# Second attention layer's edge loop: a group's sums split around the transpositions, rescaling put ahead of the key product

## Chip, cores and metric

One core of one Trainium2 chip runs the whole program in one launch. The metric is the device time of one execution in microseconds (us), smaller is better; it is given as the median of several executions. Engines are named as in the profile: PE (TensorE matmul; PEld is its weight load), DVE (VectorE), ACT (ScalarE), POOL (GpSimd), SP (SyncE and its DMA queue).

## What is computed

The program is a graph network of four residual layers over 3125 nodes of 256 features and 50,000 edges sorted by target node. The change is in the third, an attention over edges (in the kernel it is the second graph layer):

```python
qkv = (h @ W_qkv + b_qkv).reshape(n, 3, H, DH)          # H = 8 heads of DH = 32
q, k, v = (qkv[:, 0], qkv[:, 1], qkv[:, 2])
score = jnp.einsum('ehd,ehd->eh', q[dst], k[src]) * SCALE
mx = jax.ops.segment_max(score, dst, num_segments=n)
ex = jnp.exp(score - mx[dst])
denom = jax.ops.segment_sum(ex, dst, num_segments=n)
attn = ex / denom[dst]
msg = attn[:, :, None] * v[src]
h_new = jax.ops.segment_sum(msg, dst, num_segments=n)
...
return (h_out + h) @ W_out + b_out
```

## The kernel before

`attention_edges` goes over the edges in tiles of 128. Two tiles are an item, which sums into one window of 128 target nodes; two items (four tiles) are a group; there are 110 groups. Four groups are a chunk: over its 2048 edges the running maximum of the scores is made at one time, so that a chunk's weights are known only some steps after its scores. A node whose edges cross from one chunk to the next has its sums rescaled to the new maximum.

Each engine has a program of its own, written by hand as a function `step`, which `rounds` writes out once for each step i (a function `at(k)` gives the group i+k). What one engine's step does is done in exactly that order, and the engines meet at semaphores (`need` waits for several). The place of a step is i mod 4. In step i:

- POOL gathers key and value rows of group i+3 by four indirect DMAs (L1772), once the slot of group i-7 has been summed.
- ACT copies the two window sums of group i-8 out of PSUM (`keep`, L1787; the second copy waits for the first), with the gather indices of group i+4 (L1816) between the two copies; then it makes the one-hot matrix of group i+3 (L1826, L1828: distance, then a ramp) and turns the transposed one-hot of group i+2 into the operand `a_spread` (L1833). At place 2 it spreads the weights (`weights`, L1801) and copies the factor of growth (L1836); at place 1 it takes the exponentials (L1840, L1842).
- PE makes the queries of the edges of group i+1 (the query products, L1898 and L1899, two for each of four tiles; they need `a_spread`), transposes the one-hot of group i+2 (L1912), and sums group i-7 (`add_group`): it clears two PSUM banks with products of zeros (L1862) and adds four tiles (L1865). The sums wait for the group's messages (`s_msg`) and for both copies of the group summed one step earlier (`s_acc`), because the banks change owner. Ahead of the last tile's query products stands one small product of the chunk (`chunk_rows`): at place 0 the transposition of the scores (L1873), at place 1 the carries (L1877), at place 2 the transposition of the exponentials (L1881). Behind the transpositions stand at place 0 the tails (L1917, which needs DVE's ends, L1964) and at place 2 the growth (L1921). At place 3 the group summed is the first of its chunk, and the sums wait for DVE's rescaling too (`s_rs`).
- DVE multiplies queries and keys of group i (key product, L2005), then reduces the products to scores (L2018), and weights the values of group i-6 (messages, L1954). The chunk's scans stand between (L1962 to L1964 and L1971 to L1973 at place 0, L1980 to L1986 at place 1). At place 3 the rescaling (L1993, L1995) stands behind the key product; it works on a PSUM bank and waits for the copies of the group summed one step earlier.

At each end, POOL, ACT and PE run a few steps with less work (filling, and draining the last eight groups).

Of the kernel before, what the change touches and what calls it, by code (L numbers as in the profile page):

```python
# [283 lines left out]
def real(g):  # L284

    return not isinstance(g.n, int) or 0 <= g.n < g.COUNT
# [1419 lines left out]
def attention_edges(c, A):  # L1706
# [10 lines left out]
    with ExitStack() as s:  # L1717
# [21 lines left out]
        bank = lambda w: ap[:, bass.ds(w & 1, 1), 0:DM].rearrange("p a d -> p (a d)")  # L1739
        other = lambda w: ap[:, bass.ds((w + 1) & 1, 1), 0:DM].rearrange("p a d -> p (a d)")  # L1740
        hT = c.ps("a_hotT", [P, IG * P], F32, s)
# [11 lines left out]
        with nc.Block() as block:  # L1753
# [23 lines left out]
            def _(act):  # L1777
# [28 lines left out]
                def step(at):  # L1806
                    i = at(0)
                    a = at(-SUM - 1)
                    if real(a):
                        wins = item_windows(act, c, a.n)  # L1810
                        keep(a, 0, wins[0])
                    g = at(4)
                    if real(g):

                        need(act, s_ag, (s_rows[g.slot], g.turn * 64))
                        nc.scalar.copy(idx[:, g.slot, :], c.src_i[:, bass.ds(g.n * IG, IG)]).then_inc(s_idx, 1)  # L1816
                    if real(a):
                        keep(a, 1, wins[1])
                    if i.place == 2 and closed(i.chunk - 1):
# [31 lines left out]
            def _(pe):  # L1851
# [4 lines left out]

                def add_group(m, both):

                    wins = both >> 1, (both + 1) >> 1
                    need(pe, None, (s_msg, m.n + 1), (s_acc, m.n * JG), *([(s_rs, 2 * m.chunk + 2)] if m.place == 0 else []), own=True)  # L1860
                    for w in [p for p in previous] + [wins[0]]:
                        mm(other(w)[:, 0:2], none[:, :], none[:, 0:2], start=True, stop=False, skip_group_check=True)  # L1862
                    previous[:] = [wins[1]]
                    for j in range(IG):
                        last = mm(bank(wins[j // CT]), hot[:, hots(m, j), :], rows[:, m.slot * IG + j, D:ROW], start=False, stop=False, skip_group_check=True)  # L1865
                    last.then_inc(s_agg, 1)

# [15 lines left out]
                def step(at):  # L1883
                    i = at(0)
                    ch = i.chunk - 1
                    m = at(-SUM)
                    sums = ahead.take(i.step, "sums", m.n) if real(m) else None
                    g = at(1)
                    if real(g):

                        both = ahead.take(i.step, "q", g.n)
                        wins = both >> 1, (both + 1) >> 1
                        need(pe, None, (s_sp, g.n + 1), (s_pr, g.n - 1), own=True)
                        for j in range(IG):
                            if j == IG - 1:
                                chunk_rows(i, ch)
                            both_parts = window(c.qhl, wins[j // CT])
                            mm(qp[g.pair][:, j * D:(j + 1) * D], spread[:, g.pair, j, :], both_parts[:, 0:D], start=True, stop=False)  # L1898
                            last = mm(qp[g.pair][:, j * D:(j + 1) * D], spread[:, g.pair, j, :], both_parts[:, D:2 * D], start=False, stop=True)  # L1899
                        last.then_inc(s_q, 1)  # L1900
                    else:
                        chunk_rows(i, ch)
                    if real(at(2)):
                        ahead.fetch(i.then, "q", at(2).n)
# [3 lines left out]
                    if real(h):  # L1908
# [4 lines left out]
                        last.then_inc(s_ht, 1)  # L1913
                    if i.place == 0 and closed(ch):

                        need(pe, None, (s_en, ch + 1), own=True)
                        mm(tails, c.rows_of_head[:, :], ends[:, :, :].rearrange("p a t -> p (a t)"), start=True, stop=True).then_inc(s_tl, 1)  # L1917
                    if i.place == 2 and closed(ch):
# [3 lines left out]
                    if real(m):  # L1922
                        add_group(m, sums)
                pe.wait_ge(s_none, 1)
# [4 lines left out]
            def _(dve):  # L1929
# [67 lines left out]
                def step(at):  # L1997
                    i = at(0)
                    m = at(-LAG)
                    ch = i.chunk - 1  # L2000
                    if real(i):

                        need(dve, s_dg, (s_q, i.n + 1), (s_rows[i.slot], (i.turn + 1) * 64))
                        keys = rows[:, four(i), 0:D]
                        v.tensor_tensor(keys, qp[i.pair][:, :].rearrange("p (a d) -> p a d", a=IG), keys, ALU.mult).then_inc(s_pr, 1)  # L2005
# [4 lines left out]
                    if i.place == 1 and closed(ch):  # L2010
                        chunk_peaks(ch)
                    if i.place == 3 and closed(ch):
                        rescale(i, ch)
                    if real(m) and i.place != 2:
                        message(m)
                    if real(i):
                        need(dve, s_dg, (s_pr, i.n + 1))
                        v.tensor_reduce(sc[:, i.cslot, i.place * IG:(i.place + 1) * IG, :].rearrange("p t h -> p (t h)"),  # L2018
                                        rows[:, four(i), 0:D].rearrange("p t (h d) -> p t h d", h=H), AX.X, ALU.add).then_inc(s_sc, 1)
                    if real(m) and i.place == 2:  # L2020
                        message(m)
                    if i.place == 0 and closed(ch):
# [464 lines left out]
```

## Time and profile before

| What | us |
|---|---|
| Median of 3 runs | 2123.23 |
| Lowest and highest run | 2111.26 and 2154.74 |
| The profiled execution, its own time | 2139.3 |
| Span of its trace | 2137.6 |
| Sums (L1865), first and last start | 1283.0 and 1901.5 |
| Key products (L2005), first and last start | 1245.8 and 1850.1 |

Busy shares of the whole span are PE 82%, DVE 70%, ACT 54% and POOL 53%. They are means over phases with different limits and say little here; the phase of the change is read for itself. All times in the trace are us from the start of the span. A row of the timeline gives the start, the busy time, the engine, the line, what is written from what, and in brackets how long the engine had been idle before it and what ended that. Ends of matmuls are modelled, so one PE row can reach a little into the next.

### The profile page before, as it was taken

The page shows a single profiled execution, that of the slowest core. Times are in us where ns is not written, and L with a number is a line of the kernel's source. Part 1 is how long each engine was busy: PE and PEld are TensorE (multiplying, and loading weights), DVE is VectorE, ACT ScalarE, POOL GpSimd, SP SyncE. Part 2 cuts the span into 40 slices and gives each one's busy share as a digit, 9 for nine tenths or more (in the row PEclk, how much of TensorE's full clock was granted, in tenths as well). Part 3 has the DMA queues.
Part 4 walks back from the last instruction along what each step waited for, and adds up shares of the span by engine and source line. Part 5 has one row for each costly group of instructions (what it writes and reads, how often), then busy time and mean ns, then how long its engine had stood idle before and what let it go on. Part 6 is the DMA issues. An engine that isn't in the chain of part 4 may idle for free. (4 is left out here: it accounts for less than half of the span.)

```text
span 2137.6 us, 44266 instructions
## 1 busy us (share of the span) xinstructions
PE 1752.7 (82%) x10497; PEld 1546.7 (72%) x10498; DVE 1487.7 (70%) x3008; ACT 1145.9 (54%) x2630; POOL 1130.8 (53%) x1194
## 2 busy tenths in 40 slices
PE   3699999999999989828974958888888888766268
PEld 3499999999999969718963747766766766645267
DVE  4388888888888845544545848889887777637722
ACT  1677777777777726403421255666665555326133
POOL 0376666666666601562443667777776666312012
PEclk7799999999999989759986959999998888767589
DMA  2443333333333312233323667677766666323310
GB/s 93 135 120 106 107 108 104 107 108 104 107 108 104 100 31 82 73 121 103 117 72 109 208 188 198 199 201 202 203 190 185 175 176 179 100 64 118 128 48 29
DMA packets 132555, 267.74 MB, mean 125 GB/s; under 512 B 24029, under 2 KB 75887, under 8 KB 132406
## 3 DMA queue, kind: packets, MB, share of 16 engines
q0 software_dynamic: 63456, 191.61, 30.8%
q1 hardware_dynamic: 68534, 73.21, 11.0%
q8 instruction: 64, 1.05, 0.2%
q10 hardware_dynamic: 416, 1.18, 0.2%
q14 instruction: 85, 0.70, 0.1%
HBM read 225.34 MB, written 42.50 MB: 125 GB/s over the span
## 5 line engine op out<-in xcount | busy, mean ns | idle before, releaser
L319 POOL DMA_INDIRECT e_rows<-h_table,e_idx x440 | 452.3, 1028 | 216.7 <-issue 107.3
L1772 POOL DMA_INDIRECT a_rows<-kv_table,a_idx x440 | 435.2, 989 | 173.9 <-issue 170.6
L1865 PE MATMUL a_agg<-a_rows,x 128*128 128x264 f32 x880 | 271.0, 460 | 0.1
L619 PE MATMUL e_w<-w2h,e_hidl 128*128 128x256 f32 x880 | 248.4, 305 | 2.9 <-DVE e_msg L704 2.9
L589 PE MATMUL e_agg<-e_msg,e_hot 128*128 128x256 f32 x880 | 246.7, 403 | 0.0
L620 PE MATMUL e_w<-w2l,e_hidh 128*128 128x256 f32 x880 | 227.1, 280 | 0.0
L1787 ACT COPY sums<-a_agg x220 | 83.3, 379 | 261.1 <-PE a_agg L1865 229.4
L1865 PEld LDWEIGHTS a_agg<-a_rows,x 128*128 128x128 f32 x880 | 182.7, 218 | 35.4
L704 DVE TENSOR_TENSOR e_msg<-e_w,e_rows 128x1024 f32<-128x1024 f32 x110 | 134.7, 1225 | 94.8 <-PE e_w L623 94.8
L619 PEld LDWEIGHTS e_w<-w2h,e_hidl 128*128 128x128 f32 x880 | 166.4, 189 | 14.6 <-issue 5.2
L623 PE MATMUL e_w<-w2h,e_hidh 128*128 128x256 f32 x880 | 175.3, 280 | 0.0
L639 ACT COPY sums<-e_agg x220 | 80.8, 367 | 173.0 <-PE e_agg L589 173.0
L620 PEld LDWEIGHTS e_w<-w2l,e_hidh 128*128 128x128 f32 x880 | 166.4, 189 | 6.1
L1898 PE MATMUL a_q<-q_parts,a_spread 128*128 x440 | 162.2, 388 | 8.5 <-ACT a_spread L1833 7.0
L1954 DVE TENSOR_TENSOR a_rows<-a_rows 128x256 f32<-128x256 f32 x440 | 156.8, 416 | 6.2 <-ACT a_rows L1801 5.7
L589 PEld LDWEIGHTS e_agg<-e_msg,e_hot 128*128 128x128 f32 x880 | 151.0, 191 | 11.7
L2005 DVE TENSOR_TENSOR a_rows<-a_q,a_rows 128x1024 f32<-128x1024 f32 x110 | 133.0, 1209 | 28.0 <-DMA a_rows<-kv_table,a_idx 23.0
L1826 ACT ACTIVATE a_apart<-iota_n,dst_rel 128x128 f32<-128x128 f32 x440 | 140.5, 394 | 0.0
L674 DVE TENSOR_TENSOR e_hidl<-e_hid,e_hidh 128x1024 fp32r<-128x1024 f32 x110 | 135.0, 1227 | 3.4
L2018 DVE TENSOR_REDUCE a_sc<-a_rows 128x32 f32<-128x1024 f32 x110 | 133.3, 1212 | 5.1 <-DVE a_rows L2005 1.1
L691 DVE SCALAR_TENSOR_TENSOR e_hid<-e_soft,e_z 128x1024 f32<-128x1024 f32 x110 | 133.1, 1210 | 5.3 <-ACT e_soft L659 5.3
L623 PEld LDWEIGHTS e_w<-w2h,e_hidh 128*128 128x128 f32 x880 | 135.2, 189 | 0.0
(461 smaller groups left out, 4512.2 us busy)
## 6 DMA issues: line engine op xcount, KB each, us to landing
e_ea<-in_eaT SPq DMA_DIRECT2D x220, 64.0 KB
m_rows<-expert_rows SPq DMA_DIRECT2D x32, 272.0 KB, 2.7
e_rows<-h_table,e_idx POOLq DMA_INDIRECT x440
a_rows<-kv_table,a_idx POOLq DMA_INDIRECT x440, 3.7
q_ab<-expert_out SPq DMA_DIRECT2D x50, 128.0 KB
kv_table<-q_kv SPq DMA_DIRECT2D x25, 256.0 KB, 2.2
u_stage<-in_m_w SPq DMA_DIRECT2D x16, 256.0 KB
x<-in_x SPq DMA_DIRECT2D x1, 3200.0 KB, 14.9
```

What stands on the lines that cost most here:

```text
L319: c.nc.gpsimd.indirect_dma_start(out=rows[:, g.slot8, j, :], out_offset=None, in_=table, in_offset=bass.IndirectOffsetOnAxis(ap=idx[:, g.s ...
L589: last = mm(bank(wins[j]), hot[:, g.slot4, t, :], msg[:, g.slot4, t, :], start=False, stop=False, skip_group_check=True)
L619: mm(w, hidl[:, g.slot, cols[k]], w2h[:, k, :], start=(k == 0), stop=False)
L620: mm(w, hidh[:, g.slot4, cols[k]], w2l[:, k, :], start=False, stop=False)
L623: last = mm(w, hidh[:, g.slot4, cols[k]], w2h[:, k, :], start=False, stop=(k == KC - 1))
L674: low = lambda to, x, h: v.tensor_tensor(to, x, h.bitcast(F32), ALU.subtract)
L704: v.tensor_tensor(msg[:, g.slot4, :, :], wp[:, :].rearrange("p (a d) -> p a d", a=IG), rows[:, g.slot8, :, :], ALU.mult).then_inc(s_msg, 1)
L1772: nc.gpsimd.indirect_dma_start(out=rows[:, g.slot * IG + j, 0:2 * D], out_offset=None, in_=c.kv_dram, in_offset=bass.IndirectOffsetOnAxis( ...
L1826: nc.scalar.activation(apart[:, j, :], c.iota_n[:, :], ACT.Abs, bias=c.dst_rel[:, bass.ds(g.n * IG + j, 1)], scale=-1.0).then_inc(s_ap, 1)
L1865: last = mm(bank(wins[j // CT]), hot[:, hots(m, j), :], rows[:, m.slot * IG + j, D:ROW], start=False, stop=False, skip_group_check=True)
L1898: mm(qp[g.pair][:, j * D:(j + 1) * D], spread[:, g.pair, j, :], both_parts[:, 0:D], start=True, stop=False)
L1954: last = v.tensor_tensor(values, values, ex, ALU.mult)
```

## The change

On PE, `add_group` becomes `add_items`, which can do the first item's two tiles, the second's, or both. At places 0, 1 and 2 the clears and the first item's sums now stand between the query products and the transpositions, and the second item's sums behind them. The wait for messages and copies (`group_ready`) goes along, and stands ahead of the last tile's query products. At place 0 the tails move behind the transpositions to directly ahead of the second item's sums. At place 3 all sums stay behind the transpositions. On DVE the rescaling of place 3 stands ahead of the key product, and at place 2 the messages stand ahead of the reduction, as at the other places. On ACT the gather indices are copied ahead of both sum copies.

```diff
 # ACT, step
+                    g = at(4)
+                    if real(g):
+                        need(act, s_ag, (s_rows[g.slot], g.turn * 64))
+                        nc.scalar.copy(idx[:, g.slot, :], ...).then_inc(s_idx, 1)
                     a = at(-SUM - 1)
                     if real(a):
                         wins = item_windows(act, c, a.n)
-                        keep(a, 0, wins[0])
-                    g = at(4)
-                    ...
-                    if real(a):
-                        keep(a, 1, wins[1])
+                        for j in range(JG):
+                            keep(a, j, wins[j])
 # PE
+                def group_ready(m):
+                    need(pe, None, (s_msg, m.n + 1), (s_acc, m.n * JG), own=True)
+                def add_items(m, both, items, tails_of):
+                    wins = both >> 1, (both + 1) >> 1
+                    held = wins[0] & 1, wins[1] & 1
+                    if 0 in items:
+                        emptied = previous + [(wins[0] + 1) & 1]
+                        previous[:] = [(wins[1] + 1) & 1]
+                        if m.place == 0:
+                            pe.wait_ge(s_rs, 2 * m.chunk + 2)
+                        for b in emptied:
+                            mm(at_bank(b)[:, 0:2], none[:, :], none[:, 0:2], start=True, stop=False, skip_group_check=True)
+                    if tails_of is not None:
+                        chunk_tails(tails_of)
+                    for j in [j for t in items for j in range(t * CT, (t + 1) * CT)]:
+                        last = mm(at_bank(held[j // CT]), hot[:, hots(m, j), :], rows[:, m.slot * IG + j, D:ROW], start=False, stop=False, skip_group_check=True)
+                    if 1 in items:
+                        last.then_inc(s_agg, 1)
 # PE, step
+                    first_now = real(m) and m.place != 0
                         for j in range(IG):
                             if j == IG - 1:
                                 chunk_rows(i, ch)
+                                if first_now:
+                                    group_ready(m)
                             ...
+                    if first_now:
+                        add_items(m, sums, [0], None)
                     ...
                     if real(m):
-                        add_group(m, sums)
+                        if not first_now:
+                            group_ready(m)
+                        add_items(m, sums, [1] if first_now else [0, 1], tails_of)
+                    elif tails_of is not None:
+                        chunk_tails(tails_of)
 # DVE, step
+                    if i.place == 3 and closed(ch):
+                        rescale(i, ch)
                     if real(i):
                         ...
-                    if i.place == 3 and closed(ch):
-                        rescale(i, ch)
-                    if real(m) and i.place != 2:
+                    if real(m):
                         message(m)
                     if real(i):
                         ...
-                    if real(m) and i.place == 2:
-                        message(m)
```

Engine PE at place 0, before, from the last tile's query products on. `m_rows4` and `m_out0` are the names under which the listing has the semaphores of the messages (`s_msg`) and of the copies (`s_acc`); `a_ends` is set by DVE's ends, and L343 loads the next windows' numbers.

```order
L1873 MATMUL a_misc<-ident,a_sc 128x128 [waits a_grown,e1_acc]
L1898 MATMUL a_q<-q_parts,a_spread 128x256
L1899 MATMUL a_q<-q_parts,a_spread 128x256
...
L1912 MATMUL a_hotT<-ident,x 128x128 [waits e1_w,e1_hidhigh]
L1912 MATMUL a_hotT<-ident,x 128x128 x3
L1917 MATMUL a_misc<-a_ends,rows_of_head 8x32 [waits a_ends]
L1862 REGISTER_ALU [waits m_out0,m_rows4]
...
L1865 MATMUL a_agg<-a_rows,x 128x264 x2
```

The same place with the change:

```order
L1888 MATMUL a_misc<-ident,a_sc 128x128 [waits a_grown,e1_acc]
L1916 MATMUL a_q<-q_parts,a_spread 128x256 [waits m_out0,m_rows4]
L1917 MATMUL a_q<-q_parts,a_spread 128x256
L1875 REGISTER_ALU x2
...
L1879 MATMUL a_agg<-a_rows,x 128x264 x2
...
L1934 MATMUL a_hotT<-ident,x 128x128 [waits e1_w,e1_hidhigh]
L1934 MATMUL a_hotT<-ident,x 128x128 x3
L1859 MATMUL a_misc<-a_ends,rows_of_head 8x32 [waits a_ends]
...
L1879 MATMUL a_agg<-a_rows,x 128x264 x2
```

The wait for messages and copies moved up past the four transpositions and the last pair of query products, and the tails moved down past half of the sums.

Engine DVE from the key product of place 2 to the reduction of place 3, before (`a_ex` is set by the spread weights, `a_grown` by ACT's copy of the growth):

```order
L2005 TENSOR_TENSOR a_rows<-a_q,a_rows 128x4x256 [waits e1_msg,e1_rows4]
...
L2018 TENSOR_REDUCE a_sc<-a_rows 128x32 [waits e1_agg]
L1954 TENSOR_TENSOR a_rows<-a_rows 128x256 [waits a_ex]
L1954 TENSOR_TENSOR a_rows<-a_rows 128x256 x3
L2005 TENSOR_TENSOR a_rows<-a_q,a_rows 128x4x256 [waits e1_msg,e1_rows5]
L1993 REGISTER_ALU [waits a_grown,m_out0]
...
L1993 SCALAR_TENSOR_TENSOR a_agg<-a_grown,a_agg 128x256
```

The same stretch with the change:

```order
L2030 TENSOR_TENSOR a_rows<-a_q,a_rows 128x4x256 [waits e1_msg,e1_rows4]
...
L1977 TENSOR_TENSOR a_rows<-a_rows 128x256 [waits a_ex]
L1977 TENSOR_TENSOR a_rows<-a_rows 128x256 x3
L2041 TENSOR_REDUCE a_sc<-a_rows 128x32 [waits e1_agg]
L2016 REGISTER_ALU [waits a_grown,m_out0]
...
L2016 SCALAR_TENSOR_TENSOR a_agg<-a_grown,a_agg 128x256
...
L2030 TENSOR_TENSOR a_rows<-a_q,a_rows 128x4x256 [waits e1_msg,e1_rows5]
```

The rescaling, with its wait for the copies, moved ahead of a key product, and the messages of place 2 ahead of a reduction.

## Rows read from the trace of the kernel before

**Rows 1.** Windows: us, busy us of PE, PEld, DVE, ACT, POOL; PEclk; DMA share; GB/s.

```profile
1292.90:1850.10 557.20, 474.80 (x2395) 387.33 (x2394) 464.90 (x1003) 330.98 (x1041) 393.46 (x397) 0.92 0.67 189
1611.30:1826.40 215.10, 184.05 (x866) 150.00 (x865) 167.47 (x362) 120.91 (x380) 144.60 (x145) 0.86 0.63 178
1754.00:1756.00 2.00, 2.00 (x6) 1.46 (x6) 1.70 (x5) 0.00 (x0) 0.49 (x1) 0.50 0.76 184
1771.00:1773.00 2.00, 2.00 (x6) 1.46 (x6) 1.34 (x2) 0.00 (x0) 0.82 (x1) 0.50 0.70 193
```

**Rows 2.** Line L1993, one rescaling per chunk, in the first two stretches of rows 1.

```profile
L1993 DVE SCALAR_TENSOR_TENSOR a_agg<-a_grown,a_agg x25: 414/429/430, 1304.5 to 1839.6; 128x256 f32 x25
L1993 DVE SCALAR_TENSOR_TENSOR a_agg<-a_grown,a_agg x9: 414/428/430, 1624.9 to 1815.9; 128x256 f32 x9
```

**Rows 3.** Waits of PE, 1283 to 1905: us in total, times, longest.

```profile
PE a_agg L1862 <- DVE a_agg L1995: 36.7, 28, 2.8
PE a_misc L1917 <- DVE a_ends L1964: 24.1, 27, 1.6
```

**Rows 4.** Timeline, PE and ACT, a step of place 1.

```profile
1482.87 0.47 PE L1898 MATMUL a_q<-q_parts,a_spread 128*128 x1
1483.30 0.28 PE L1898 MATMUL a_q<-q_parts,a_spread 128*128 x1
1484.36 0.38 ACT L1787 COPY sums<-a_agg  x1 [0.28 <-issue]
1484.62 0.63 PE L1912 MATMUL a_hotT<-ident,x 128*128 128x128 f32 x4
1485.18 0.27 PE L1862 MATMUL a_agg<-a_none 128*128 128x2 f32 x1
1485.82 2.04 PE L1865 MATMUL a_agg<-a_rows,x 128*128 128x264 f32 x8
```

**Rows 5.** Timeline, PE and ACT, the next step, of place 2.

```profile
1487.50 0.48 PE L1898 MATMUL a_q<-q_parts,a_spread 128*128 x1
1488.99 0.38 ACT L1787 COPY sums<-a_agg  x1 [0.28 <-issue]
1489.82 0.38 PE L1921 MATMUL a_misc<-a_diag,a_first 8*128 8x8 f32 x2
```

**Rows 6.** Timeline, PE, ACT and DVE, the step of place 3.

```profile
1492.45 0.48 PE L1898 MATMUL a_q<-q_parts,a_spread 128*128 x1
1493.48 1.22 DVE L2005 TENSOR_TENSOR a_rows<-a_q,a_rows 128x1024 f32<-128x1024 f32 x1
1493.98 0.38 ACT L1787 COPY sums<-a_agg  x1 [0.20 <-issue]
1494.73 0.43 DVE L1993 SCALAR_TENSOR_TENSOR a_agg<-a_grown,a_agg 128x256 f32 x1
1495.68 0.62 PE L1862 MATMUL a_agg<-a_none 128*128 128x2 f32 x2 [1.03 <-DVE a_agg L1995]
```

**Rows 7.** Timeline, PE and ACT, the step of place 0 and the next start.

```profile
1499.43 0.38 ACT L1787 COPY sums<-a_agg  x1 [0.27 <-issue]
1500.68 0.23 PE L1917 MATMUL a_misc<-a_ends,rows_of_head 128*8 128x32 f32 x2 [0.90 <-DVE a_ends L1964]
1501.12 0.61 PE L1862 MATMUL a_agg<-a_none 128*128 128x2 f32 x2 [0.21 <-issue]
1503.37 0.48 PE L1898 MATMUL a_q<-q_parts,a_spread 128*128 x1
```

**Rows 8.** Timeline, draining: the second copy and the rescaling behind it.

```profile
1889.65 0.38 ACT L1787 COPY sums<-a_agg  x1 [0.37 <-ACT sums L1787]
1890.40 0.43 DVE L1993 SCALAR_TENSOR_TENSOR a_agg<-a_grown,a_agg 128x256 f32 x1 [4.43 <-issue]
```

**Rows 9.** Timeline, filling: the spread and the query product waiting for it.

```profile
1249.24 0.58 ACT L1833 CAST a_spread<-a_hotT 128x512 fp32r<-128x512 f32 x1 [1.25 <-PE a_hotT L1912]
1250.02 0.58 PE L1898 MATMUL a_q<-q_parts,a_spread 128*128 x1 [0.93 <-ACT a_spread L1833]
```

More of the change, by code:

```diff
@@ L1739, in attention_edges @@
         bank = lambda w: ap[:, bass.ds(w & 1, 1), 0:DM].rearrange("p a d -> p (a d)")
-        other = lambda w: ap[:, bass.ds((w + 1) & 1, 1), 0:DM].rearrange("p a d -> p (a d)")
+        at_bank = lambda b: ap[:, bass.ds(b, 1), 0:DM].rearrange("p a d -> p (a d)")
         hT = c.ps("a_hotT", [P, IG * P], F32, s)
@@ L1807, in step @@
                     i = at(0)
-                    a = at(-SUM - 1)
-                    if real(a):
-                        wins = item_windows(act, c, a.n)
-                        keep(a, 0, wins[0])
                     g = at(4)
@@ L1816, in step @@
                         nc.scalar.copy(idx[:, g.slot, :], c.src_i[:, bass.ds(g.n * IG, IG)]).then_inc(s_idx, 1)
+                    a = at(-SUM - 1)
                     if real(a):
-                        keep(a, 1, wins[1])
+                        wins = item_windows(act, c, a.n)
+                        for j in range(JG):
+                            keep(a, j, wins[j])
                     if i.place == 2 and closed(i.chunk - 1):
@@ L1855, in _, with chunk_tails @@
                 previous = []
-                def add_group(m, both):
-                    wins = both >> 1, (both + 1) >> 1
[L1860 to L1866, printed above, removed]
+                def chunk_tails(ch):
+                    need(pe, None, (s_en, ch + 1), own=True)
+                    mm(tails, c.rows_of_head[:, :], ends[:, :, :].rearrange("p a t -> p (a t)"), start=True, stop=True).then_inc(s_tl, 1)
+                def group_ready(m):
+                    need(pe, None, (s_msg, m.n + 1), (s_acc, m.n * JG), own=True)
+                def add_items(m, both, items, tails_of):
+                    wins = both >> 1, (both + 1) >> 1
+                    held = wins[0] & 1, wins[1] & 1
[12 more added lines that the diff above has]
+                        last.then_inc(s_agg, 1)
                 def chunk_rows(i, ch):
@@ L1902, in step @@
                         chunk_rows(i, ch)
+                        if first_now:
+                            group_ready(m)
+                    if first_now:
+                        add_items(m, sums, [0], None)
                     if real(at(2)):
@@ L1913, in step @@
                         last.then_inc(s_ht, 1)
-                    if i.place == 0 and closed(ch):
-                        need(pe, None, (s_en, ch + 1), own=True)
-                        mm(tails, c.rows_of_head[:, :], ends[:, :, :].rearrange("p a t -> p (a t)"), start=True, stop=True).then_inc(s_tl, 1)
+                    tails_of = ch if i.place == 0 and closed(ch) else None
                     if i.place == 2 and closed(ch):
@@ L1922, in step @@
                     if real(m):
-                        add_group(m, sums)
+                        if not first_now:
+                            group_ready(m)
+                        add_items(m, sums, [1] if first_now else [0, 1], tails_of)
+                    elif tails_of is not None:
+                        chunk_tails(tails_of)
                 pe.wait_ge(s_none, 1)
```

## Prediction

> **What bounds the kernel now.** I first read the busy time by stretches. From the key product at 1292.9 to the one at 1850.1 the trace has 557.20 us [rows 1], and in it 25 rescalings, one per chunk [rows 2]: 22.29 us a chunk on average. That mean hides two kinds of chunk. In the nine chunks from 1611.3 to 1826.4 [rows 1, 2] a chunk takes 215.10 / 9 = 23.90 us, and PE's granted clock is 0.86 on average. As the clock has only the levels 1.2 and 2.4 GHz, 0.86 means 28% of the time at the lower one, 6.7 us of each chunk; the reader sees two such stretches, at 1754 and at 1771, with PE busy all the time at 0.50 [rows 1]. An undisturbed chunk, from the query products of one place 1 to those of the next, takes 1503.37 - 1482.87 = 20.50 us [rows 4, 7]. So a chunk with two falls of the clock costs 3.40 us more than one with none, 1.70 us a fall.
>
> Next come PE's waits. In this phase it waits 36.7 us for the rescaling (28 times) and 24.1 us for the ends (27 times) [rows 3]. These two are what the change goes for. To see whether removing them shortens a chunk I read the timeline of one undisturbed chunk, step by step. There a third wait shows that has no line of its own in the list of waits: at place 1 the second copy out of PSUM ends at 1484.36 + 0.38 = 1484.74, and the first clear starts at 1485.18, 0.44 behind it [rows 4]. The query products and the transpositions (1484.62 to 1485.18) just fill the time until the copies are done. So the loop from the sums over the two copies to the next sums is already closed at this place; all PE work in front of the clears is free because it lies under the copies.
>
> **The change part by part.** No computation is added or removed; only order and waits change.
>
> *First item ahead of the transpositions, places 0, 1, 2.* The wait for the copies now stands ahead of the last pair of query products. What lay under the copies, that pair and the four transpositions, comes behind them. I count one step from the end of the second copy, at the full clock, with these pieces: from a copy's end to a waiting query product 0.20 us (from the spread's end, 1249.24 + 0.58 = 1249.82, to the product at 1250.02 [rows 9]); a pair of products at the head of a stream 0.43 (1482.87 to 1483.30); clears 0.64 (1485.18 to 1485.82); all four tiles of sums 1.68 (1485.82 to 1487.50), so 0.84 an item; transpositions 0.56 [rows 4, 5].
>
> - Place 1: 1484.74 + 0.20 + 0.43 + 0.64 + 0.84 + 0.56 + 0.84 = 1488.25, where the next step started at 1487.50 before: 0.75 later. But the next query products also need the spread of these transpositions, which now come late. They start at 1486.85 and end 0.63 later [rows 4] at 1487.48; in the filling steps, where PE has nothing else, it is idle for 0.93 us between the transpositions and the query product that needs their spread [rows 9]. That gives 1488.41, 0.91 later, and it is the later one that counts.
> - Place 2: the second copy ends at 1488.99 + 0.38 = 1489.37 [rows 5]. With the growth between (0.38) the step ends at 1489.37 + 0.20 + 0.43 + 0.64 + 0.84 + 0.56 + 0.38 + 0.84 = 1493.26, against 1492.45 [rows 6]: 0.81 later. The spread is no later than this.
> - Place 0: the copy ends at 1499.81; with the tails, 1500.68 to 1501.12 or 0.44 [rows 7], the step ends at 1499.81 + 0.20 + 0.43 + 0.64 + 0.84 + 0.56 + 0.44 + 0.84 = 1503.76, against 1503.37: 0.39 later. Here the old wait of 0.90 for the ends does go: DVE's ends come before 1500.68, and PE is at the tails only at about 1502.5. Most of the gain is eaten by what now follows the copies.
>
> *Rescaling ahead of the key product, place 3.* The key product ended at 1493.48 + 1.22 = 1494.70 and the rescaling started at 1494.73, so it looks as if the key product held it. But the second copy ended at 1493.98 + 0.38 = 1494.36, and 0.37 later is 1494.73 [rows 6]. In the draining steps, where no key product stands in between, the rescaling starts 0.37 behind the copy too (1889.65 + 0.38 = 1890.03, then 1890.40 [rows 8]). So the copy holds it, the move gains nothing here, and the wait of 1.03 us on PE stays: 0. The key product itself, 1.22 us, now lies behind the rescaling; the scores' transposition at place 0 gets later by at most that, mostly under the new wait for the copies. That wait is at least 0.78 us: at place 1, three pairs at 0.43 from 1482.87 end at 1484.16, and PE goes on at 1484.94. So 0.44 at most can stick out; I take 0 and keep 0.44 for the bounds. Without that cover it would be the whole 1.22.
>
> *Messages of place 2 ahead of the reduction, indices ahead of the copies.* Both 0. The weights they need are spread on ACT right behind the second copy (1489.37), while DVE's key product of place 2 runs; the index copy leaves a gap on ACT that the second copy cannot use, since it is held by the first one (0.37 idle there without an index copy [rows 8]). POOL's gathers get their semaphore a little earlier and still wait for the end of the sums. Filling and draining steps are left as they are: there the sums already wait for copies.
>
> Sum for a chunk at the full clock: 0.91 + 0.81 + 0 + 0.39 = 2.11, so 22.61 us. The bounds: the step after the copies may take 0.44 as before the clears instead of 0.20, which adds 3 x 0.24 = 0.72 (23.33, and 23.77 with the 0.44 above); or the last pair may be hidden wholly, which takes off 3 x 0.43 = 1.29 (21.32). I take 0.20, since there a query product waits for ACT, as it now will.
>
> *The clock.* PE's waits before were two, near each other, at places 3 and 0. Now there are four, one in each step: the old 1.03 at place 3, and some 0.8 us at each of the other places. In the late stretch the clock fell twice a chunk with two waits hardly larger than these; in the undisturbed chunk it did not fall. Spread evenly, each wait is alone, but there are more. I take one fall a chunk, between the none of the undisturbed chunk and the two of the late ones, at 1.70 us: 22.61 + 1.70 = 24.31.
>
> On this the row shows PE at 0.50 at 1771, right behind a wait for the rescaling and so for a copy [rows 1]. The Trainium skill (TensorE: Matmul & The Clock Gate, section "Loop structure matters more than you think") has it that a copy out of PSUM between streams of matmuls doesn't break PE's warmth, by which there would be no falls and the first rival's time. The same page ("A second HAM failure mode: psum-queue depth-cycling") says that small idles between groups of matmuls, coming often, make the clock swing between its levels; that would give falls as in the forecast or in the second rival. The trace agrees with the second statement: 0.86 over nine chunks, with no wait on PE longer than 2.8 us.
>
> The time: 25 chunks at 24.31 are 607.8 us instead of 557.2, so 50.6 more. On the profiled execution's 2139.3 us (its span of 2137.6 and 1.7 around it, which stay) that is 2190 us. The runs shown have a median of 2123.23, some 16 us under the profiled one; as the new phase is built up from its own chunks and not from the mean of before, I stay with 2190.
>
> **Rivals.**
>
> 1. *No falls.* The waits are short and far apart, and the clock stays full. Then a chunk is 22.61, 25 are 565.3, 8.1 more: 2147 us, between 2115 (21.32 a chunk) and 2176 (23.77). For it: the undisturbed chunk had waits of 1.03 and 0.90 at the full clock. Against it: the nine late chunks had hardly longer ones and fell twice each.
> 2. *Two falls a chunk.* The waits come at every step and the late stretch's pattern holds throughout: 22.61 + 3.40 = 26.01, 25 are 650.3, 93.1 more: 2232 us.
> 3. *Not slower: the copies are not what ends last.* If the copies ended 0.8 us or more earlier against PE's products than in the timeline [rows 4, 5, 7], the moved wait would find them done; the ends' wait of 0.90 would be gone, and without the pair of waits the clock would stay full. Then every chunk is 20.50 or a little less, 25 are 512.5, 44.7 less: 2095 us. For it speaks that both waits it goes for are large [rows 3]. Against it: the clear at 1485.18 stands 0.44 behind the copy, so the copies have no slack at all. It decides from the point where the second copy ends before the third tile's products do.
>
> **How the numbers follow.** The forecast, about one fall a chunk, gets 0.45; no falls 0.25; two or more falls 0.18; the copies in time 0.12. The time given is 2190 us. The range 2125 to 2240 takes in most of the first rival and the second rival, and leaves out the third and what is beyond two falls. About 2% can be told from no change in this kernel: against 2123 that is 2081 to 2166. Slower: the forecast nearly whole (0.42) and the second rival, 0.60. Within 2%: the first rival, the rest of the forecast and two thirds of the third, 0.36. Faster: 0.04.
>
> **What would show it.** In the profile after, the timeline of a chunk should show the last pair of query products starting some 0.2 us behind the second copy at places 0, 1 and 2, with PE idle for 0.8 us or more before it; a new entry in PE's waits, query products (L1916) for ACT's copies; the entry of the tails for the ends gone; the rescaling still some 0.37 behind the second copy. The chunk should be 22 to 23 us where the clock stays full. The forecast is wrong if query products do not wait there, if an undisturbed chunk is 20.5 us or less, or if the falls come four times a chunk or not at all.

## The result, and the profile after

The median is 2175.86 us (2174.38 to 2178.78, 4 runs), beside 2127.45 for the kernel before on the same chip: a ratio of 1.0224 [1.0165, 1.0282]. In brackets stands the 95% interval of a ratio. It is slower; whether by 2% or more the interval leaves open. The profiled execution took 2175.47 us, its span is 2173.7, so 36.1 us more than before. The first row below is the window between the same two key products as in [rows 1], the second one undisturbed chunk, from the query products of place 1 to the next of place 1.

```profile
1288.40:1886.90 598.50, 482.17 (x2390) 366.35 (x2390) 461.31 (x1003) 337.63 (x1041) 399.39 (x398) 0.96 0.62 176
1480.68:1503.86 23.18, 18.40 (x99) 14.01 (x97) 18.47 (x40) 13.77 (x42) 15.94 (x17) 1.00 0.62 182
```

The phase grew from 557.20 to 598.50 us, 41.3 more; it starts 4.5 us earlier, and what comes behind it is 0.7 shorter: 36.1. A chunk takes 598.50 / 25 = 23.94 us on average, with 24.31 predicted. The mean clock rose from 0.92 to 0.96 all the same, so the loss is in the order. The nine chunks at the full clock average 23.41 us (before: 20.59, also nine), the sixteen others 24.24.

The waits of PE in this phase, as in [rows 3]:

```profile
PE a_q L1916 <- ACT sums L1787: 51.1, 76, 1.1
PE a_hotT L1934 <- issue: 31.9, 93, 0.6
PE a_agg L1875 <- DVE a_agg L2018: 27.2, 27, 2.8
```

The ends' 24.1 us are gone from the list. In their place the query products wait 51.1 us for the copies, 76 times, and the wait for the rescaling has stayed. The second row was not predicted: before the transpositions PE is idle 93 times with nothing to wait for ("issue").

The timeline of place 1 in the undisturbed chunk, PE and ACT, answers to [rows 4]; the last four rows are places 2 and 0 ([rows 5, 7]):

```profile
1480.68 0.44 PE L1916 MATMUL a_q<-q_parts,a_spread 128*128 x1
1482.13 0.38 ACT L1787 COPY sums<-a_agg  x1 [0.37 <-ACT sums L1787]
1482.65 0.36 PE L1916 MATMUL a_q<-q_parts,a_spread 128*128 x1 [0.61 <-ACT sums L1787]
1482.97 0.61 PE L1875 MATMUL a_agg<-a_none 128*128 128x2 f32 x2
1483.53 1.15 PE L1879 MATMUL a_agg<-a_rows,x 128*128 128x264 f32 x4
1485.10 0.63 PE L1934 MATMUL a_hotT<-ident,x 128*128 128x128 f32 x4 [0.42 <-issue]
1486.65 0.38 PE L1916 MATMUL a_q<-q_parts,a_spread 128*128 x1
...
1489.32 1.15 PE L1879 MATMUL a_agg<-a_rows,x 128*128 128x264 f32 x4
1490.83 0.63 PE L1934 MATMUL a_hotT<-ident,x 128*128 128x128 f32 x4 [0.36 <-ACT x L1827]
...
1500.89 1.15 PE L1879 MATMUL a_agg<-a_rows,x 128*128 128x264 f32 x4
1502.31 0.63 PE L1934 MATMUL a_hotT<-ident,x 128*128 128x128 f32 x4 [0.26 <-issue]
```

The second copy ends at 1482.13 + 0.38 = 1482.51 and the waiting query product starts 0.14 later, after 0.61 us of idle time. From the start of the first item's sums to the transpositions it is 1485.10 - 1483.53 = 1.57 us at place 1, 1.51 at place 2 and 1.42 at place 0, where the prediction had 0.84. (At place 2 the trace names ACT's one-hot, L1827, as what came last, at 1489.86 + 0.63 = 1490.49; the loads of that step, of the kind shown below for the other two, close at 1490.6. Over the phase the one-hot is named 6 times, for 2.2 us.) What fills that time is on PE's sequencer. L343, a helper, loads the next step's window numbers into registers; the code has it between the first item's sums and the transpositions. Its rows in this chunk's place 1, then at place 0 (durations in ns, first and last start in us):

```profile
L343 PEldq TENSOR_LOAD <-g_row x2: 298/300/302, 1483.5 to 1484.3; - x2
L343 PEldq FUSED_REGOPS  x2: 151/151/151, 1483.9 to 1484.7; - x2
L343 PEldq SEQ_ASSERT  x2: 18/18/18, 1484.1 to 1484.9; - x2
...
L343 PEldq TENSOR_LOAD <-g_row x2: 296/298/301, 1500.9 to 1501.6; - x2
```

And in the kernel before, at place 1 of [rows 4]:

```profile
L343 PEldq TENSOR_LOAD <-g_row x2: 301/302/302, 1483.2 to 1483.9; - x2
L343 PEldq FUSED_REGOPS  x2: 151/151/151, 1483.6 to 1484.2; - x2
```

Before, the two loads ran from 1483.2 to about 1484.4, while the query products ran and the copies were pending (the second ended at 1484.74): hidden. After, the sequencer stands at the moved wait until 1482.51, so the loads start only at 1483.5 and end at 1484.9, and the transpositions behind them start at 1485.10. Before, "issue" ahead of the transpositions was 11.7 us in 38 times.

At place 3 the rescaling answers to [rows 6]:

```profile
1493.99 0.38 ACT L1787 COPY sums<-a_agg  x1 [0.37 <-ACT sums L1787]
1494.74 0.43 DVE L2016 SCALAR_TENSOR_TENSOR a_agg<-a_grown,a_agg 128x256 f32 x1 [3.51 <-ACT sums L1787]
1495.73 0.61 PE L1875 MATMUL a_agg<-a_none 128*128 128x2 f32 x2 [0.83 <-DVE a_agg L2018]
```

It starts 0.37 behind the copy as before, though no key product stands in front of it now; DVE is idle 3.51 us ahead of it.

### The profile page after: what moved, and what is told of

Same layout as the page of the kernel before. It is cut to its first block and busy times, and to the rows that moved or that the text cites. A ratio compares the mean times of both kernels' runs of the same rounds, so it can differ in the third digit from the quotient of the medians.

```text
span 2173.7 us, 44266 instructions
## 1 busy us (share of the span) xinstructions
PE 1754.3 (81%) x10497; PEld 1522.3 (70%) x10498; DVE 1481.4 (68%) x3008; ACT 1153.4 (53%) x2630; POOL 1138.1 (52%) x1194
## 5 line engine op out<-in xcount | busy, mean ns | idle before, releaser
L1772 POOL DMA_INDIRECT a_rows<-kv_table,a_idx x440 | 440.0, 1000 | 208.1 <-issue 205.1
L1916 PE MATMUL a_q<-q_parts,a_spread 128*128 x440 | 147.3, 356 | 62.3 <-ACT sums L1787 51.1
L1879 PEld LDWEIGHTS a_agg<-a_rows,x 128*128 128x128 f32 x880 | 169.4, 210 | 29.0 <-issue 0.2
L589 PEld LDWEIGHTS e_agg<-e_msg,e_hot 128*128 128x128 f32 x880 | 149.9, 190 | 11.5
L1916 PEld LDWEIGHTS a_q<-q_parts,a_spread 128*128 128x128 f32 x440 | 90.1, 205 | 90.6 <-issue 85.7
```

Of the source, the lines that this page charges most:

```text
L589: last = mm(bank(wins[j]), hot[:, g.slot4, t, :], msg[:, g.slot4, t, :], start=False, stop=False, skip_group_check=True)
L1772: nc.gpsimd.indirect_dma_start(out=rows[:, g.slot * IG + j, 0:2 * D], out_offset=None, in_=c.kv_dram, in_offset=bass.IndirectOffsetOnAxis( ...
L1879: last = mm(at_bank(held[j // CT]), hot[:, hots(m, j), :], rows[:, m.slot * IG + j, D:ROW], start=False, stop=False, skip_group_check=True)
```

## The experiments

The kernel before ran on the chip of each set: 2133.04 (first four runs), 2126.51 (next four), 2133.63 (last three). All ratios are to it unless said otherwise. The change itself was not run again beside them, so its 2175.86 us is from another set of runs. Where a run is given as a share of the change, times of two sets are divided. A chunk counts as one at the full clock if its granted clock is 0.99 or more from the key product of one place 1 to the next.

**PE's part alone.** `add_items`, the moved wait and the tails as in the change; ACT and DVE as before.

```diff
 # against the change: ACT, step
-                        for j in range(JG):
-                            keep(a, j, wins[j])
+                        keep(a, 0, wins[0])
...
+                        keep(a, 1, wins[1])
 # DVE, step
-                    if i.place == 3 and closed(ch):
-                        rescale(i, ch)
...
-                    if real(m):
+                    if i.place == 3 and closed(ch):
+                        rescale(i, ch)
+                    if real(m) and i.place != 2:
                         message(m)
...
+                    if real(m) and i.place == 2:
+                        message(m)
```

> PE's part of the change alone; ACT and DVE in the old order. Theory 1 (the wait for the copies, moved ahead of the last pair of query products, is the whole loss): as the full change, 1.018 to 1.027 of the kernel before, an undisturbed chunk 23.2 to 23.8 us, PE's query products waiting some 50 us for ACT's copies. Theory 2 (DVE loses: its key product and scores come late behind the rescaling): most of the loss gone, 1.000 to 1.008.

Measured: 2176.61 us, 1.0208 [1.0137, 1.0280]; full-clock chunks 23.04, mean 23.98; PE waits 50.5 us for the copies. In the time, PE's part is the whole loss. A full-clock chunk is a little shorter than I had expected, and 0.37 shorter than in the full change.

**The rest alone.** The order of ACT (indices ahead of both copies) and DVE as in the change, PE as before.

```diff
 # DVE, step
+                    if i.place == 3 and closed(ch):
+                        rescale(i, ch)
...
-                    if i.place == 3 and closed(ch):
-                        rescale(i, ch)
-                    if real(m) and i.place != 2:
+                    if real(m):
                         message(m)
...
-                    if real(m) and i.place == 2:
-                        message(m)
 # ACT, step: as in the change
```

> ACT's and DVE's part of the change alone (indices ahead of the copies, rescaling ahead of the key product, messages ahead of the reduction at place 2); PE in the old order. Theory 1: 0.995 to 1.005 of the kernel before, the rescaling still 0.37 us behind the second copy, PE's wait for the rescaling still about 1 us each time. Theory 2: 1.010 to 1.022. A third view (the key product held the rescaling): PE's wait for the rescaling down by half or more, 0.98 to 0.99.

Measured: 2147.15 us, 1.0056 [1.0024, 1.0088]; the two full-clock chunks of its profile 21.12. The profiled execution is the slowest of the ten, 2159.97. PE's wait for the rescaling is 34.2 us in 27 times, hardly less than the 36.7 before, so the key product did not hold the rescaling. A small loss, not the nothing that I had put down; the run on the rescaling below goes into it.

**Loads early.** The change, with PE's loads of the next step's windows moved ahead of the wait, so that they run under it. `fetch_next` holds the four lines taken out below.

```diff
                             if j == IG - 1:
+                                fetch_next()
                                 chunk_rows(i, ch)
...
                         add_items(m, sums, [0], None)
-                    if real(at(2)):
-                        ahead.fetch(i.then, "q", at(2).n)
-                    if real(at(1 - SUM)):
-                        ahead.fetch(i.then, "sums", at(1 - SUM).n)
```

> The full change, with PE's loads of the next step's window numbers moved from between the first item's sums and the transpositions to ahead of the wait for the copies. Theory 1a (the 0.6 to 0.7 us per step by which the new step is longer than predicted is PE's queue executing these loads behind the wait): the gap between the first item's last sum and the transpositions falls from about 0.7 us to under 0.2, an undisturbed chunk from 23.4 to 21.4 to 22.2 us, 0.975 to 0.988 of the full change. Theory 1b (the transpositions wait for something else there, such as ACT's one-hot): 0.995 to 1.005 of the full change, the gap stays.

Measured: 2145.46 us, 1.0052 [1.0021, 1.0083], so 2145.5 / 2175.9 = 0.986 of the change. Full-clock chunks 21.87 instead of 23.41. A place 0 at the full clock, then the loads in the step behind it:

```profile
1492.45 0.36 PE L1922 MATMUL a_q<-q_parts,a_spread 128*128 x1 [0.78 <-ACT sums L1787]
1493.36 1.15 PE L1879 MATMUL a_agg<-a_rows,x 128*128 128x264 f32 x4
1494.35 0.60 PE L1937 MATMUL a_hotT<-ident,x 128*128 128x128 f32 x4
1497.62 0.40 PE L1892 MATMUL a_misc<-carried,heads_of_row 8*128 8x34 f32 x2 [0.72 <-issue]
...
L343 PEldq TENSOR_LOAD <-g_row x2: 300/301/302, 1496.3 to 1497.0; - x2
```

The first item takes 0.99 us to the transpositions, not 1.42. The loads run while the copies are pending (the second ends at 1497.71 in that step), and "issue" now stands ahead of the chunk's product. This one line of order is worth 1.54 us of a chunk's 2.82 of growth.

**Tails alone.** The kernel before; only the tails move, from ahead of the clears to between the two items' sums.

```diff
                     for j in range(IG):
+                        if j == CT and tails_of is not None:
+                            chunk_tails(tails_of)
                         last = mm(bank(wins[j // CT]), ...)
...
-                    if i.place == 0 and closed(ch):
-                        need(pe, None, (s_en, ch + 1), own=True)
-                        mm(tails, ...).then_inc(s_tl, 1)
+                    tails_of = ch if i.place == 0 and closed(ch) else None
```

> The kernel before, with only the tails of place 0 moved: from ahead of the clears to between the two items' sums; nothing goes ahead of the transpositions. Theory 1: the wait for the ends (24 us in all) goes without anything new in its place, and the clock falls less often, as the pair of waits is broken up: 0.975 to 0.992 of the kernel before. Rival (DVE's own chain sets the chunk, 20.5 us at best, and the falls come from the wait for the rescaling alone): 0.995 to 1.003.

Measured: 2105.93 us, 0.9886 [0.9816, 0.9955]; mean chunk 21.22, full-clock chunks 20.72, seventeen of them instead of nine. The ends' wait is gone, the rescaling's is unchanged:

```profile
1286.80:1817.40 530.60, 448.61 (x2390) 362.56 (x2390) 463.10 (x1003) 332.51 (x1040) 401.36 (x398) 0.97 0.70 199
...
PE a_agg L1867 <- DVE a_agg L2001: 35.2, 27, 2.8
```

A full-clock chunk is no shorter than before (20.59): what is gained is the clock, 0.97 for 0.92. One of the two waits that stood near each other is gone; that the falls are fewer for this reason is an argument here, and the next run tests it. So one part of the change pays by itself. Whether it still does beside the others was not tried.

**Before, with PE kept busy.** The transpositions of places 0 and 3, just ahead of the two waits, are done three times.

```diff
+                        for again in range(3 if i.place in (0, 3) else 1):
                             for j in range(IG):
                                 last = tr(hT[:, j * P:(j + 1) * P], ...)
```

> The kernel before, with the four transpositions of places 3 and 0 done three times in a row instead of once; same values, 16 additional transpositions a chunk that lie where PE would wait for the rescaling and for the ends. Theory C (the late stretch's 23.9 us a chunk come from the clock, and the clock falls because of PE's idle time at these two places): the time at the lower clock in the 25 chunks falls from some 90 us to under 25, all chunks at 20.4 to 21.0 us, 0.978 to 0.988 of the kernel before. Rival D (transpositions don't count for the clock, or the falls have another cause): low time as before, 0.998 to 1.010.

Measured: 2097.00 us, 0.9880 [0.9813, 0.9947]. The clock is full in 24 of the 25 chunks, the mean chunk 20.74:

```profile
1281.30:1799.70 518.40, 477.74 (x2787) 398.39 (x2786) 465.00 (x1002) 330.24 (x1041) 393.53 (x398) 1.00 0.70 203
```

PE's idle time at the two waits fell from 36.7 to 8.5 us (rescaling) and from 24.1 to 4.4 (ends). Only filler was added, and the falls are gone: in the kernel before, PE's idle time at these waits caused them. The two places were filled together, so this run does not tell which of them counts for more.

**The change, with PE kept busy.** The third tile's query products are done three more times ahead of the wait, at places 0 to 2.

```diff
                                 if first_now:
+                                    for again in range(3):
+                                        mm(qp[g.pair][:, (j - 1) * D:j * D], ...)
+                                        mm(qp[g.pair][:, (j - 1) * D:j * D], ...)
                                     group_ready(m)
```

> The full change, with the third tile's query products repeated three times at places 0, 1 and 2 just ahead of the wait for the copies; same values, filling PE's new idle time of about 0.7 us. Theory C: the time at the lower clock in the 25 chunks falls from 51 us to under 20, the mean chunk from 23.94 to about 23.4 (what an undisturbed one takes already), 0.990 to 0.996 of the full change, so still 1.010 to 1.020 of the kernel before: the order, not the clock, is most of the loss. Rival D: low time unchanged, 0.998 to 1.006 of the full change.

Measured: 2171.90 us, 1.0224 [1.0156, 1.0292], so 0.998 of the change (by their two ratios to the kernel before, 1.000). That is in the rival's range and not in the one forecast. PE's wait for the copies fell from 51.1 to about 1 us, full-clock chunks rose from nine to fifteen, and still they take 23.36 us:

```profile
1286.90:1882.80 595.90, 527.95 (x2840) 413.55 (x2840) 462.27 (x1001) 337.30 (x1039) 395.39 (x398) 0.97 0.62 177
...
PE a_hotT L1937 <- issue: 31.5, 94, 0.6
PE a_agg L1875 <- DVE a_agg L2021: 27.0, 27, 2.8
```

Ten chunks are still disturbed, more than I had expected; PE's waits for the rescaling and for the loads, the last two rows, are left, which may be why. But most of the time lost is not the clock's: with the clock fuller, the chunk stays as long.

**Wait behind the last pair.** The change, with the wait behind the last pair of query products, and the loads between that pair and the wait.

```diff
-                                if first_now:
-                                    group_ready(m)
...
                         ahead.fetch(i.then, "sums", at(1 - SUM).n)
+                    if first_now:
+                        group_ready(m)
+                        add_items(m, sums, [0], None)
```

> The full change, with the wait for messages and copies moved behind the last pair of query products, and PE's loads of the next window numbers between that pair and the wait. Theory 1: pair (0.32 us a step) and loads (about 0.6) come back under the copies, only clears, first item and transpositions stay behind: an undisturbed chunk 21.0 to 21.7 us, 0.972 to 0.986 of the full change, 0.995 to 1.006 of the kernel before. Rival (the loads alone mattered): not under 21.8 us a chunk, as with the loads moved.

Measured: 2148.58 us, 1.0104 [1.0023, 1.0184]; full-clock chunks 22.44, longer than expected and on the rival's side of 21.8. What is missing is at the wait. A second copy and the clears behind it, in the timeline of ACT and PE, then the loads of that step:

```profile
1465.43 0.38 ACT L1787 COPY sums<-a_agg  x1 [0.37 <-ACT sums L1787]
1466.62 0.61 PE L1875 MATMUL a_agg<-a_none 128*128 128x2 f32 x2 [1.16 <-ACT sums L1787]
...
L343 PEldq TENSOR_LOAD <-g_row x2: 294/298/302, 1464.9 to 1465.5; - x2
L343 PEldq SEQ_ASSERT  x2: 18/18/18, 1465.5 to 1466.1; - x2
```

From the copy's end (1465.81) to the clears it is 0.81 us, in the two steps behind it 0.44 and 0.59, while a query product waiting at the same semaphore starts after 0.14. Two things make up the difference. The loads start only behind the last pair and here close at 1466.1, some 0.35 after the copy, so part of them still sticks out. And the clears have register instructions of their own behind the wait: these are the 0.44 that is left where the loads end before the copy, as at the next wait.

**Rescaling alone.** The kernel before, with only the rescaling ahead of the key product.

```diff
+                    if i.place == 3 and closed(ch):
+                        rescale(i, ch)
                     if real(i):
...
-                    if i.place == 3 and closed(ch):
-                        rescale(i, ch)
```

> The kernel before with nothing but the rescaling moved ahead of the key product. Theory R (with PE's old order, where no new wait covers it, the 0.6 % that the ACT and DVE parts cost is the key product and the scores behind it coming late): 1.003 to 1.009 of the kernel before, an undisturbed chunk 21.0 us. Rival (the messages of place 2 or the indices cost it): 0.998 to 1.002, an undisturbed chunk 20.5 us.

Measured: 2138.08 us, 1.0028 [1.0004, 1.0053]; full-clock chunks 21.05, 0.46 longer than before. In the old order of PE the key product behind the rescaling is late for what follows: in a full-clock chunk the tails of place 0 start 1459.15 - 1455.87 = 3.28 us into the step, against 1500.68 - 1497.94 = 2.74 in the kernel before. By the time the loss is 4.5 us, where 25 x 0.46 would be 11.5; in the profiles 13 chunks of 25 were disturbed instead of 16. As PE's part alone (2176.61) and the whole change (2175.86) agree, no cost of the move shows in the time under the new wait. Their full-clock chunks (23.04 and 23.41) leave up to some tenths of a us open.

**Short copy.** The change, with a shorter second copy.

```diff
+                    lo = D if j == 1 else 0
-                    nc.scalar.copy(window(c.sums, w)[:, 0:DM], bank(w)).then_inc(s_acc, 1)
+                    nc.scalar.copy(window(c.sums, w)[:, lo:DM], ap[...]).then_inc(s_acc, 1)
```

> The full change, with the second copy out of PSUM cut from 264 to its last 8 columns, so that most of the second item's sums are left out of the result. The copy lasts about 0.17 instead of 0.38 us and nothing else changes. Theory 1 (the loop from the sums over both copies to the next sums sets the step): 0.2 us less a step, an undisturbed chunk 0.7 to 0.9 us shorter, 22.5 to 22.8 us, 0.985 to 0.994 of the full change. Rival (PE's own work, or the spread, sets it): a chunk within 0.2 us of 23.4, 0.998 to 1.002.

Measured: 2157.23 us, 1.0128 [1.0082, 1.0175], so 0.991 of the change; full-clock chunks 22.74, which is 0.67 less; PE's wait for the copies 40.4 us. The copy is 0.17 instead of 0.38 us, 0.21 shorter. It counts in all four steps, since at place 3 the rescaling waits for it, so 0.84 could be gained. Counted from PE's query products, the steps of the full-clock chunks are on average 0.10, 0.17, 0.17 and 0.13 shorter at places 1, 2, 3 and 0, 0.57 in all by these borders of a chunk. So a chunk follows the end of the second copy, though not to the full length: PE's waits for ACT's one-hot, 2.2 us in the change, are 7.0 here.

**Tails alone, with filler.** Two ways to hold the clock on top of the moved tails: the third tile's query products four more times at place 3, or the transpositions of place 3 three times.

```diff
+                                for again in range(4 if i.place == 3 and real(m) else 0):
+                                    mm(qp[g.pair][:, (j - 1) * D:j * D], ...)
 # the other
+                        for again in range(3 if i.place in (3,) else 1):
```

> The kernel before with the tails between the two items' sums, as in the earlier run, and at place 3 the third tile's query products repeated four times while PE would wait for the rescaling; same values. Theory C: the wait for the rescaling is what still makes the clock fall there; the mean chunk goes from 21.2 to 20.5 us, low time in the 25 chunks under 10 us, 0.975 to 0.986 of the kernel before. Rival D: as without the repetition, 0.985 to 0.992.

> The kernel before with the tails between the two items' sums, and at place 3 the four transpositions done three times while PE would wait for the rescaling; same values. Theory C: no falls are left between the filling and the draining steps (low time in the 25 chunks under 8 us), the mean chunk 20.4 to 20.7 us, 0.980 to 0.988 of the kernel before. Rival (DVE's chain of 20.5 us and more is all that is left, and the two steps don't add up): 0.987 to 0.991, as each of them alone.

Measured: 2101.51 us, 0.9888 [0.9821, 0.9954], with the query products, and 2100.63 us, 0.9865 [0.9831, 0.9900], with the transpositions. The mean chunks are 21.08 and 20.93 (tails alone: 21.22), at the full clock 20.77 and 20.80. The first run is in its rival's range; both mean chunks are longer than expected, with five and three chunks disturbed. The second has the lowest ratio of all, 1.35% under the kernel before, but by the intervals no filler is told apart from the tails alone.

## Why the prediction was right, and where its terms were off

It said slower, 2190 us, range 2125 to 2240; it is 2175.86. The mechanism is the one named: the wait for the copies out of PSUM moved ahead of work that had lain under them, and that work came behind it. "No slack at all" holds at place 1, where it was read; at place 0 the first clear stood at 1501.12, 1.31 behind the copy's end and not 0.44, and the prediction's sum for that step has this in it. Products waiting some 0.2 us behind the copy, their new entry in PE's waits, the ends' entry gone and the rescaling 0.37 behind the copy all show as stated. Two terms were mis-sized, in opposite directions: the chunk at the full clock came out 0.80 longer, its clock term 1.17 smaller. That the mean chunk, 23.94, came within 0.37 of 24.31 is so in part luck.

- *The chunk at the full clock*: 22.61 predicted, 23.41 measured. The term that was off is "0.84 an item", from the first item's sums to the transpositions: it took 1.42 to 1.57. The prediction counted matmuls and left out the two register loads that stand in that place of the program. From the copy's end to the transpositions it had 0.20 + 0.43 + 0.64 + 0.84 = 2.11; it was 2.59, 2.53 and 2.46 at places 1, 2 and 0, although wake-up, pair and clears came out shorter (0.14, 0.32, 0.56 at place 1). Moving the loads away took 1.54 us off a chunk. Over whole steps it is place 1 that misses most: the steps grew by 1.34, 0.90, -0.01 and 0.45 us at places 1, 2, 3 and 0, against 0.91, 0.81, 0 and 0.39.
- *The spread chain* at place 1: 0.93 predicted between transpositions and next query product; 1485.10 + 0.63 = 1485.73 to 1486.65 is 0.92.
- *The clock*: 1.70 us a chunk predicted, 23.94 - 23.41 = 0.53 measured. Sixteen of 25 chunks were disturbed, not all, and a disturbed one was 24.24 - 23.41 = 0.83 longer, not 1.70. That waits spread over the chunk make fewer falls than two near each other was weighed and not carried far enough. That a fall costs less where PE waits for copies in every step fits these numbers, but no run isolated it.
- *Rescaling*: the gain was rightly put at nothing, since the copy holds it. The 0 for its cost holds for the time of the changed kernel, by PE's part alone, where the new wait can cover the later scores. Without that cover, in the old order, the move costs 0.46 a full-clock chunk, not the whole 1.22.
- *Indices and messages* were not tried apart. The three together gave 1.0056 in the old order of PE, the rescaling by itself 1.0028, with intervals that overlap; in the new order the three together cost nothing that shows.
- *The ends*: the old wait did go. That this alone gains 1.1%, by the clock, was not priced as a part of the change: the sum has 0.90 us of one step for it, and the clock only as a whole.
- *The rivals*: copies in time is out (query products waited 76 times), two falls a chunk too. No falls at 2147 had the chunk too short and is out by the clock.

Not tried: taking away the second copy's wait for the first (0.37 idle between them), since both may write the same window.

## What to carry to other kernels

Before a wait is moved ahead of work, list all that its engine did under it, its register loads too: behind the wait the sequencer cannot run ahead, and what was free is then on the path. Splitting a group's sums into two halves gained nothing here, as the event that opens them comes last. And where an engine stands idle often and briefly, look at the clock of that stretch before counting the idle time: moving one small product, or repeating work nobody waits for, gained 1.1 to 1.4% here with a full-clock chunk that was no shorter.

## What the runs showed of the hardware

- PE's sequencer takes about 0.7 us for one window number (a load of 0.30, register operations of 0.15, and gaps): two starting at 1483.5 ended at 1484.9. At place 1 of the kernel before they ran under query products, and PE had no idle time from them; behind the moved wait they show as "issue" idle on the next matmul, up to 0.6 us each time.
- A query product waiting for ACT's copy started 0.14 us after its end; clears with register instructions behind the same wait 0.44 after it where the loads were done by then (1473.50 - 1473.06), and 0.81 where the loads were still running (1466.62 - 1465.81).
- Repeated transpositions held the clock: with three times the four at two places the window's clock went from 0.92 to 1.00. The Trainium skill (TensorE: Matmul & The Clock Gate, Part 4 on the PE-mode transpose) has it that a transposition doesn't count as busy PE for the clock in the way a matmul does. Here the fillers were transpositions alone, standing among matmuls, and they held the clock, so the measurement goes against it for this kernel. The rows call them plain matmuls and do not show the mode, so whether they are the page's case stays open.
